# First and last routed expert stage: the two-round loop over experts written out over all units, with waits on constants

## The chip, the cores and the metric

The kernel runs on one core of one Trainium2 chip. The metric is the device time of one execution in microseconds (us), the median of several. The engines are named as the profile names them: PE is TensorE (matmul), PEld its weight loads, ACT is ScalarE, DVE is VectorE, POOL is GpSimd, SP is SyncE, which here only issues DMAs.

## What is computed

Four layers, each a cross attention and a gated feed-forward part. The change touches the feed-forward parts of the first and the last layer (L0 and L3), both mixtures of experts with two experts for each of 2048 tokens of 128 numbers. Cut to what matters, of the first (slots per expert: 640, experts: 8, hidden size 512):

```python
xe = zeros((E, cap + 1, D)).at[experts, pos_safe].set(xf[tokens])[:, :cap]
h = silu(einsum('ecd,edf->ecf', xe, W1)) * einsum('ecd,edf->ecf', xe, W3)
ye = einsum('ecf,efd->ecd', h, W2)
out = zeros((T, D)).at[tokens].add(wk[:, None] * ye[experts, ...])
```

and of the last (256 slots, 16 experts, hidden size 512):

```python
xin = einsum("tec,td->ecd", dispatch, xt)
h = gelu(einsum("ecd,edf->ecf", xin, fc1_w) + fc1_b[:, None, :], approximate=False)
eout = einsum("ecf,efd->ecd", h, fc2_w) + fc2_b[:, None, :]
```

## The kernel before

The whole network is one program. Its stages run one behind the other; each is a block in which every engine has its own list of instructions, engines wait for each other by counting semaphores, and a block ends when all engines have come to its end. `routed_experts` is the first routed stage (names `L0f_...`) and the last (`L3f_...`). The second one (`L2f_...`, function `block_experts`) is written another way and is not touched: straight code over 39 units, waits on constants.

A routed stage begins with the head (`lead`): gating, choosing experts, and sending every token's row to its expert's slots in DRAM (`slots`) by indirect DMAs of POOL. Then come the experts. An expert's slots are T tiles of 128 rows: five in the first stage, cut into units of three and of two tiles (`chunks=[3, 2]`), and two in the last, one unit (`chunks=[2]`). Weights and rows of U experts lie in SBUF at a time: U is 4 of 8 experts in the first stage, 8 of 16 in the last. The loop (`Fori`) over experts therefore makes two rounds, with U experts, and `UC` = 8 units, in its body. In both stages that is 16 units in all.

For a unit PE does three things, in functions of their names:

- `turn` (L2557): transposes the unit's rows into `psT`; ACT copies them into `xsT` (`turned`, L2513; in the last stage with scale and bias);
- `hidden` (L2566): for each of J = 4 column blocks one matmul into `psA`, in the first stage a second one into `psB` for the gate; ACT applies SiLU or GELU from `psA` into `h` (L2533), and in the first stage DVE multiplies `h` by `psB` (`gate`, L2617). `psA` and `psB` have two banks each, so the third column block waits until ACT has read the first (`a_free`);
- `outputs` (L2581): J matmuls for each tile into `psY`; DVE copies the result into `ys` (L2634, or with the bias L2632) and the rows' home addresses into `home` (L2630); POOL sends each tile of `ys` to its place in `results` by an indirect DMA (L2664).

Within a round these are pipelined by hand: PE issues unit k+2's `turn` and unit k+1's `hidden` ahead of unit k's `outputs`. The round starts with `turn(0)`, `turn(1)`, `hidden(0)` and ends with the `outputs` of its last two units, since `k + 2 < UC` and `k + 1 < UC` bound the pipeline to the body:

```python
for k in range(UC):
    if k + 2 < UC:
        turn(k + 2)
    if k + 1 < UC:
        hidden(k + 1)
    outputs(k)
```

Every wait in the body counts to a number that depends on the round (`i * UC + (k + 1)`), which each engine works out in a register. POOL's indirect DMAs follow a dummy multiply into `waited` (L2674), which waits for `y_free` (the copy) and for POOL's own counter `turn`. DVE's copy of a unit waits until the rows of the unit two before it have returned (`returned`), since `ys` has two buffers. SP loads the next round's rows and weights into an expert's place when its last unit has been copied (`y_free`, L2496 to L2498). ACT's function tables are loaded by instructions that the compiler puts in (`ACT_TABLE_LOAD`).

When all rows are back, the first stage fetches them for the next stage while PE computes the next attention's values (`Values1`); the last stage collects them and writes the output (`Collect`).

Of the kernel before, what the change touches and what calls it, by code (L numbers as in the profile page):

```python
# [18 lines left out]
P = 128  # L19
# [2396 lines left out]
def routed_experts(nc, m, name, c):  # L2416
# [6 lines left out]
    UC = U * CH  # L2423
    assert UC % 2 == 0 and UC >= 4 and EB % U == 0
    TOT = EB * CH
    NS = EB * T * P
# [9 lines left out]
    with ExitStack() as ctx:  # L2436
# [9 lines left out]
        pay, waited = c["last"] if ends else sb("pay", [P, 2, NT, PAY]), sb("waited", [P, 1])  # L2446
# [12 lines left out]
        turn = sem("turn")  # L2459
# [7 lines left out]
        N = UC * J  # L2467
# [3 lines left out]
        def _(sp):  # L2471
# [19 lines left out]
            with sp.Fori(0, EB // U - 1) as i:  # L2491
                for u in range(U):
                    at = lambda a: a[bass.ds(i * U + (U + u), 1)].rearrange(
                        "o p f -> p (o f)" if len(a.shape) == 3 else "o p j f -> p (o j) f")
# [12 lines left out]
        @block.scalar  # L2507
        def _(act):
            lead.scalar(act)
            with act.Fori(0, EB // U) as i:  # L2510
                a = Tally(N, i)

                def turned(k):  # L2513

                    tiles = units[k][2]
                    act.wait_ge(t_full, i * UC + (k + 1))

                    act.wait_ge(b_full, i * N + (k + 1) * J)
                    src, dst = psT[:, k % 2, 0:tiles * P], xsT[:, k % 2, 0:tiles * P]
                    if c.get("scale") is None:  # L2520
                        nc.scalar.copy(dst, src).then_inc(t_free, 1)  # L2521
                    else:
                        nc.scalar.activation(dst, src, ACT.Identity, bias=c["bias"], scale=c["scale"]).then_inc(t_free, 1)

                turned(0)
                turned(1)
                for k, (u, _, tiles) in enumerate(units):
                    for j in range(J):
                        if j == 0:

                            act.wait_ge(y_full, i * UC + (k + 1))
                        act.wait_ge(a_full, a.take() + (2 * J + 1))
                        nc.scalar.activation(h[:, k % 2, j, 0:tiles * P], psA[:, j % 2, 0:tiles * P], c["act"],  # L2533
                                             bias=b1s[:, u, j:j + 1] if b1 else 0.0).then_inc(a_free, 1)
                    if k + 2 < UC:
                        turned(k + 2)
                a.end()
            if values is not None:
                values.scalar(act)
            if ends:  # L2540
                collect.second(act)

        @block.tensor
        def _(pe):
# [9 lines left out]
            with pe.Fori(0, EB // U) as i:  # L2554
                a = Tally(N, i)

                def turn(k):  # L2557
                    u, first, tiles = units[k]
                    if first == 0:
                        pe.wait_ge(x_in[u], i * 16 + 16)  # L2560
                    pe.wait_ge(t_free, i * UC + (k + 1))
                    for t in range(tiles):
                        last = pe.transpose(psT[:, k % 2, t * P:(t + 1) * P], xs[:, u, first + t, 0:D], m.ident)
                    last.then_inc(t_full, 1)
# [30 lines left out]
                for k in range(UC):  # L2595
                    if k + 2 < UC:
                        turn(k + 2)
# [1293 lines left out]
```

## Time and profile before

| | us |
|---|---|
| median of 3 runs | 1281.98 |
| lowest and highest of them | 1275.63, 1286.26 |
| span of the profiled execution (no time of its own beside it) | 1279.7 |
| units of the first stage, from first transposes to last copy | 229.38 to 346.70 |
| units of the last stage, from first transposes to last copy | 1183.60 to 1260.72 |
| PE busy over the span | 1073.0 (84%) |
| DVE, ACT, POOL busy | 699.7, 600.8, 498.8 |
| mean granted clock of PE | 0.896 of full speed |

Times in the trace are counted from the span's start. Busy times are sums of an engine's instructions; PE's are modelled at their ends, since matmuls overlap. An entry in brackets behind a row is the engine's idle time before it and what ended it. In the table of stretches, each engine has its busy us and the number of its instructions.

### The profile page before, as it was taken

What the parts mean: (1) busy time and instruction counts of PE and PEld (TensorE: products, weight loads), DVE (VectorE), ACT (ScalarE), POOL (GpSimd) and SP (SyncE); (2) the same over time, 40 slices, a digit from 0 to 9 for tenths busy, and PEclk for the clock granted to TensorE, in tenths of its full rate; (3) what the DMA queues carried; (4) which work ended last, traced back from release to release, by engine and by line L of the source; (5) the groups of instructions that cost most, each with busy time, mean ns of one, the idle gap of its engine ahead of it and who ended that gap; (6) DMA issues with size and microseconds to landing.
All of it is one profiled execution on the core that took longest, in us unless ns stands there. A gap on an engine that the chain in (4) does not pass through costs nothing. (4 is left out here: it accounts for less than half of the span.)

```text
span 1279.7 us, 26365 instructions
## 1 busy us (share of the span) xinstructions
PE 1073.0 (84%) x8602; PEld 744.3 (58%) x8602; DVE 699.7 (55%) x3354; ACT 600.8 (47%) x1506; POOL 498.8 (39%) x783
## 2 busy tenths in 40 slices
PE   5999788799969999989996868994779999961983
PEld 4778565587725666664443655993644444541773
DVE  7667375233368776645465642115658888754012
ACT  3555466323257766624321432442644666631553
POOL 4767427133447565423003555551020000067343
PEclk9999799799979999998997975997876999975887
DMA  9789811131099950001660024662040222015533
GB/s 246 231 227 177 185 37 51 51 125 52 23 155 121 164 96 1 2 21 36 141 126 1 2 78 140 195 187 72 31 143 24 67 68 60 22 29 169 141 93 104
DMA packets 138791, 124.60 MB, mean 97 GB/s; under 512 B 14015, under 2 KB 112737, under 8 KB 138665
## 3 DMA queue, kind: packets, MB, share of 16 engines
q1 hardware_dynamic: 129624, 107.82, 36.7%
q0 software_dynamic: 7168, 12.83, 3.0%
q10 hardware_dynamic: 1872, 2.37, 0.5%
q8 instruction: 67, 1.10, 0.4%
q14 instruction: 60, 0.48, 0.1%
HBM read 88.12 MB, written 37.70 MB: 98 GB/s over the span
## 5 line engine op out<-in xcount | busy, mean ns | idle before, releaser
L998 ACT ACTIVATE L_Z<-L_Z,L_nmx 128x154 f32<-128x154 f32 x256 | 105.2, 412 | 47.9 <-DVE L_nmx L1071 47.7
L3592 DVE CUSTOM_DVE_ANT_0 L3s_masked<-L3s_psS,L3s_trilw 128x512 f32<-128x512 f32 (+3 forms) x256 | 109.8, 486 | 24.0 <-PE L3s_psS L3419 23.5
L347 POOL TENSOR_TENSOR L_Z<-L_Z,L_mx 128x512 f32<-128x512 f32 x84 | 87.6, 1043 | 63.9 <-DVE L_mx L722 62.0
L3547 ACT ACTIVATE L3s_E<-L3s_psT 128x512 f32<-128x512 f32 (+1 forms) x192 | 87.6, 529 | 49.2 <-PE L3s_psT L3432 49.0
L887 POOL TENSOR_TENSOR L_Z<-L_Z,L_rin 128x488 f32<-128x488 f32 x64 | 64.1, 1001 | 67.2 <-DVE L_rin L1079 67.2
L912 PE MATMUL L_psS<-L1k_G,L_xnT 128*128 128x462 f32 x192 | 84.7, 539 | 4.8 <-DVE L_nmx L1071 3.5
L722 DVE CUSTOM_DVE_ANT_0 L_Z<-L_psS,L_Z 128x154 f32<-128x154 f32 x256 | 63.4, 313 | 31.1 <-PE L_psS L403 28.6
L1071 DVE CUSTOM_DVE_ANT_0 L_Z<-L_psS,L_mask 128x154 f32<-128x154 f32 x256 | 67.7, 311 | 11.9 <-PE L_psS L912 9.4
L578 ACT ACTIVATE L_E<-L_psT 128x512 f32<-128x512 f32 x84 | 46.2, 596 | 53.7 <-PE L_psT L416 53.6
L1089 DVE COPY L_PT<-L_psT 122x512 f32<-122x512 f32 x64 | 43.7, 683 | 38.5 <-PE L_psT L922 38.2
L3389 POOL COPY L3s_VG<-L3s_V 128x236 f32<-128x236 f32 x16 | 6.1, 386 | 149.5 <-PE L3s_psO L3443 148.2
L3419 PE MATMUL L3s_psS<-L3s_KS,L3s_QS 72*128 72x512 bf16 (+3 forms) x256 | 55.6, 333 | 7.7 <-PEq L3405 4.6
L2617 DVE TENSOR_TENSOR L0f_h<-L0f_h,L0f_psB 128x384 f32<-128x384 f32 (+1 forms) x64 | 31.2, 488 | 54.2 <-PE L0f_psB L2579 50.4
L3430 PE MATMUL L3s_psT<-L3s_QS,L3s_KS 75*128 75x512 bf16 (+3 forms) x256 | 60.3, 313 | 0.0
L3443 PE MATMUL L3s_psO<-L3s_E,L3s_VG 128*32 128x128 f32 (+3 forms) x512 | 49.6, 452 | 8.3 <-ACT L3s_E L3547 8.1
L2841 POOL DMA_INDIRECT resultsL<-L2f_ys,L2f_home x39 | 38.1, 977 | 44.9 <-DVE L2f_ys L2828 44.6
L3430 PEld LDWEIGHTS L3s_psT<-L3s_QS,L3s_KS 75*128 75x128 bf16 x256 | 25.8, 101 | 44.9 <-issue 23.1
L2576 PE MATMUL L0f_psA<-L0f_xsT,L0f_w 128*128 128x256 f32 (+1 forms) x128 | 47.0, 450 | 3.4 <-ACT L0f_xsT L2521 3.4
L3432 PE MATMUL L3s_psT<-L3s_triub,L3s_identb 128*128 128x128 bf16 x256 | 48.2, 225 | 0.0
L1403 ACT ACTIVATE L1m_h<-L1m_psA 128x512 f32<-128x512 f32 x36 | 21.4, 598 | 56.6 <-PE L1m_psA L1317 56.5
L416 PE MATMUL L_psT<-const,L_Z 128*128 128x128 f32 x336 | 47.4, 287 | 0.5 <-ACT L_Er L578 0.5
L998 ACT ACTIVATION_READ_ACCUMULATOR L_Z<-L_Z,L_nmx 128x1 f32 x256 | 47.8, 187 | 0.0
(638 smaller groups left out, 2812.1 us busy)
## 6 DMA issues: line engine op xcount, KB each, us to landing
L_Z<-in_fside_Bx16xSxS SPq DMA_DIRECT2D x16, 1232.0 KB, 7.1
L2f_w<-in_L_ffn_W SPq DMA_DIRECT2D x39, 256.0 KB, 3.4
slotsL<-empty SPq DMA_DIRECT2D x1, 8320.5 KB, 75.1
L3f_w<-in_L_ffn_fc_w SPq DMA_DIRECT2D x32, 256.0 KB, 4.1
L0f_w<-in_L_ffn_W SPq DMA_DIRECT2D x24, 256.0 KB, 3.9
L1m_cb<-comb_rows SPq DMA_DIRECT2D x6, 1024.0 KB, 10.1
L3s_QS<-q_parts SPq DMA_DIRECT2D x144, 32.0 KB
L3s_KS<-k_parts SPq DMA_DIRECT2D x48, 96.0 KB
```

Of the source, the lines that this page charges most:

```text
L347: nc.gpsimd.tensor_tensor(Z[:, t % NZ, h, 0:KM_], Z[:, t % NZ, h, 0:KM_], top.broadcast_to([P, HG, KM_]), ALU.subtract).then_inc(z_ready, 1)
L722: last = nc.vector.tensor_tensor_reduce(Z[:, t % NZ, h], psS[:, j, (g % 3) * S2:(g % 3) * S2 + S2], add, 1.0, LOW, ALU.add, ALU.max, mx[:, ...
L887: nc.gpsimd.tensor_tensor(zz, zz, r.unsqueeze(2).broadcast_to([P, 4, KM]), ALU.mult).then_inc(norm_done, 1)
L912: pe.matmul(psS[:, n % 2, 0:w * S2], xnT[:, (t // 2) % 2, (t % 2) * P:(t % 2 + 1) * P], G[:, t // TB, hs].rearrange("p h k -> p (h k)"), s ...
L998: last = nc.scalar.activation(Z[:, t % 2, h], Z[:, t % 2, h], ACT.Exp, scale=-1.0, bias=nmx[:, t % 2, h:h + 1], accum_out=sums[:, t % 2, h ...
L1071: last = nc.vector.tensor_tensor_reduce(Z[:, t % 2, h], psS[:, n % 2, at:at + S2], mask[:, t % TB], 1.0, -LOW, ALU.add, ALU.min, nmx[:, t ...
L3419: last = pe.matmul(psS[:, k, at:at + wd], QS[0:TR, g.slot, h, t * P:(t + 1) * P], KS[0:TR, g.slot, h, 0:wd], start=(n == 0), stop=(n == le ...
L3430: pe.matmul(psT[:, k, at:at + wd], KS[0:TR + 3, g.slot, h, t * P:(t + 1) * P], QS[0:TR + 3, g.slot, h, t * P:S], start=(n == 0), stop=Fals ...
L3432: last = pe.matmul(psT[:, k, at:at + P], identb[:], triub[:], start=False, stop=(n == len(tiles) - 1), skip_group_check=True)
L3443: last = pe.matmul(psO[32 * h:32 * h + 32, j * P:S], VG[:, g.par, j, h * (DH + 1):h * (DH + 1) + 32], E[:, g.par, h, EO[j]:EO[j] + S - j * ...
L3547: nc.scalar.activation(E[:, g.par, h, EO[group[0]]:EO[group[0]] + wd], psT[:, k, 0:wd], ACT.Exp).then_inc(t_free, 1)
L3592: last = nc.vector.tensor_tensor_reduce(masked[:, k, at:at + wd], psS[:, k, at:at + wd], trilw[:, S - wd:S], 1.0, LOW, ALU.add, ALU.max, m ...
```

## The change

The body of the loop becomes plain code over all 16 units n of a stage: `units` runs over all experts, `e % U` names an expert's place in SBUF, the pipeline runs through (`n + 2 < TOT`), and every wait is for a constant. The dummy multiply, its tile and the counter `turn` go. SP's loads, of the same sizes under the same counts, are written out as well. The core of the diff (DVE's part changes in the same way as PE's):

```diff
-    units = [(u, sum(chunks[:q]), chunks[q]) for u in range(U) for q in range(CH)]
+    units = [(e, sum(chunks[:q]), chunks[q]) for e in range(EB) for q in range(CH)]
...
-            with sp.Fori(0, EB // U - 1) as i:
-                for u in range(U):
...
-                    sp.wait_ge(y_free, i * UC + ((u + 1) * CH + 2))
-                    sp.dma_start(xs[:, u], at(slots_in)).then_inc(x_in[u], 16)
-                    load_w(at, u)
+            for e in range(U, EB):
+                sp.wait_ge(y_free, (e - U + 1) * CH + 2)
+                sp.dma_start(xs[:, e % U], slots_in[e]).then_inc(x_in[e % U], 16)
+                load_w(lambda a: a[e], e % U)
...
-            with act.Fori(0, EB // U) as i:
-                a = Tally(N, i)
...
+            def turned(n):
+                e, _, tiles = units[n]
+                act.wait_ge(t_full, n + 1)
+                act.wait_ge(b_full, (n + 1) * J)
...
+            turned(0)
+            turned(1)
+            for n, (e, _, tiles) in enumerate(units):
+                act.wait_ge(y_full, n + 1)
+                for j in range(J):
+                    act.wait_ge(a_full, n * J + j + 2 * J + 1)
+                    nc.scalar.activation(h[:, n % 2, j, 0:tiles * P], psA[:, j % 2, 0:tiles * P], c["act"],
+                                         bias=b1s[:, e % U, j:j + 1] if b1 else 0.0).then_inc(a_free, 1)
+                if n + 2 < TOT:
+                    turned(n + 2)
...
-            with pe.Fori(0, EB // U) as i:
...
-                for k in range(UC):
-                    if k + 2 < UC:
-                        turn(k + 2)
-                    if k + 1 < UC:
-                        hidden(k + 1)
-                    outputs(k)
-                a.end()
+            turn(0)
+            turn(1)
+            hidden(0)
+            for n in range(TOT):
+                if n + 2 < TOT:
+                    turn(n + 2)
+                if n + 1 < TOT:
+                    hidden(n + 1)
+                outputs(n)
...
-            pool.sem_inc(turn, 1)
-            with pool.Fori(0, EB // U) as i:
-                for k in range(UC):
-                    pool.wait_ge(turn, i * UC + (k + 1))
-                    pool.wait_ge(y_free, i * UC + (k + 3))
-
-                    nc.gpsimd.tensor_tensor(waited[:], m.ones[:, 0:1], m.ones[:, 0:1], ALU.mult).then_inc(turn, 1)
-                    give_back(k)
+            for n, (e, first, tiles) in enumerate(units):
+                pool.wait_ge(y_free, n + 3)
...
```

Two places of the order of instructions follow. The first is ACT at the start of the first stage's units, the list of before: behind the routing's exponential come the loop's branch and the body, in which a table load stands in front of the first copy (behind the wait for the transposes, `t_full`) and one in front of the first SiLU (behind a wait for `y_full` alone).

```order
L1663 ACTIVATE L0f_e<-L0f_e 128x16 [waits L0f_diff_ready]
L2510 UNCONDITIONAL_BRANCH
L2510 ISA
L2518 ISA [waits L0f_t_full]
L2521 ACT_TABLE_LOAD
L2521 COPY L0f_xsT<-L0f_psT 128x384 [waits L0f_b_full]
L2516 REGISTER_ALU
L2518 REGISTER_ALU [waits L0f_t_full]
L2521 COPY L0f_xsT<-L0f_psT 128x256 [waits L0f_b_full]
L2532 REGISTER_ALU [waits L0f_y_full]
L2533 ACT_TABLE_LOAD
L2533 ACTIVATE L0f_h<-L0f_psA 128x384 [waits L0f_a_full]
```

The same place in the list of the change.

```order
L1663 ACTIVATE L0f_e<-L0f_e 128x16 [waits L0f_diff_ready]
L2510 COPY L0f_xsT<-L0f_psT 128x384 [waits L0f_b_full,L0f_t_full]
L2510 COPY L0f_xsT<-L0f_psT 128x256 [waits L0f_b_full,L0f_t_full]
L2520 ACT_TABLE_LOAD [waits L0f_a_full]
L2520 ACTIVATE L0f_h<-L0f_psA 128x384 [waits L0f_y_full]
L2520 ACTIVATE L0f_h<-L0f_psA 128x384 [waits L0f_a_full] x3
```

The load in front of the copies is gone; the one in front of the SiLU now waits for the first hidden result (`a_full`). The part between the branch and the loop's end was run twice, and with it its two loads. In the last stage the order is the same, with GELU.

The second place is PE at the end of the last stage's units, the list of before: the end of the loop's body, the outputs of its last two units back to back, then the branch back.

```order
L2576 MATMUL L3f_psA<-L3f_xsT,L3f_w 128x256
L2587 MATMUL L3f_psY<-L3f_w,L3f_h 128x128 x8
L2583 REGISTER_ALU
L2587 MATMUL L3f_psY<-L3f_w,L3f_h 128x128 x8
L2554 REGISTER_ALU
L2554 COMPARE_AND_BRANCH
L2436 UNCONDITIONAL_BRANCH
```

The same place in the list of the change, from the transposes of unit 15 on.

```order
L2547 MATMUL L3f_psT<-const,L3f_xs 128x128 x2
L2559 MATMUL L3f_psA<-L3f_xsT,L3f_w 128x256 x4
L2570 MATMUL L3f_psY<-L3f_w,L3f_h 128x128 x8
L2559 MATMUL L3f_psA<-L3f_xsT,L3f_w 128x256 x4
L2570 MATMUL L3f_psY<-L3f_w,L3f_h 128x128 x16
L2435 UNCONDITIONAL_BRANCH
```

Before, the sixteen output matmuls back to back stood behind units 6 and 7 and again behind units 14 and 15; now only behind units 14 and 15, and between units 7 and 8 stands what stands between any two units: transposes, a hidden layer, outputs.

## Rows read from the trace of the kernel before

**Rows 1.** Table of stretches: busy us of PE, PEld, DVE, ACT, POOL; clock, DMA share, GB/s

```profile
289.40:291.90 2.50, 0.71 (x8) 0.48 (x5) 0.49 (x2) 1.93 (x3) 1.89 (x3) 1.00 0.35 63
...
291.90:352.00 60.10, 60.10 (x330) 46.02 (x331) 20.95 (x50) 20.23 (x45) 24.25 (x32) 1.00 0.11 37
...
1192.00:1221.80 29.80, 28.89 (x194) 24.77 (x194) 3.46 (x14) 14.43 (x33) 13.91 (x20) 1.00 0.61 169
...
1221.80:1225.90 4.10, 1.19 (x6) 0.70 (x5) 0.49 (x2) 4.06 (x6) 3.14 (x5) 0.87 0.82 196
...
1225.90:1231.70 5.80, 5.80 (x15) 4.20 (x16) 0.00 (x0) 3.18 (x7) 0.22 (x1) 0.50 0.43 150
...
800.00:868.00 68.00, 68.00 (x612) 68.00 (x611) 12.52 (x72) 31.06 (x72) 34.85 (x36) 1.00 0.63 180
```

**Rows 2.** Timeline of VectorE, first stage: start, us, copies of finished units 0, 4, 8

```profile
247.40 0.55 DVE L2634 COPY L0f_ys<-L0f_psY 128x384 f32<-128x384 f32 x1
...
274.64 0.55 DVE L2634 COPY L0f_ys<-L0f_psY 128x384 f32<-128x384 f32 x1
...
303.96 0.55 DVE L2634 COPY L0f_ys<-L0f_psY 128x384 f32<-128x384 f32 x1
```

**Rows 3.** The same of the last stage: copies of units 0, 5, 8

```profile
1195.14 0.42 DVE L2632 TENSOR_TENSOR L3f_ys<-L3f_psY,L3f_b 128x256 f32<-128x256 f32 x1
...
1215.90 0.42 DVE L2632 TENSOR_TENSOR L3f_ys<-L3f_psY,L3f_b 128x256 f32<-128x256 f32 x1
...
1233.84 0.42 DVE L2632 TENSOR_TENSOR L3f_ys<-L3f_psY,L3f_b 128x256 f32<-128x256 f32 x1
```

**Rows 4.** Timeline of ACT and PE at the first stage's back edge

```profile
289.96 1.28 ACT L2521 ACT_TABLE_LOAD   x1 [4.91 <-PE L0f_psT L2563]
...
291.86 0.91 PE L2576 MATMUL L0f_psA<-L0f_xsT,L0f_w 128*128 128x384 f32 x2 [1.79 <-ACT L0f_xsT L2521]
```

**Rows 5.** Timeline of PE and ACT at the last stage's back edge

```profile
1223.71 1.13 PE L2576 MATMUL L3f_psA<-L3f_xsT,L3f_w 128*128 128x256 f32 x4 [1.87 <-ACT L3f_xsT L2523]
...
1224.05 1.28 ACT L2533 ACT_TABLE_LOAD   x1
...
1225.88 0.80 PE L2576 MATMUL L3f_psA<-L3f_xsT,L3f_w 128*128 128x256 f32 x1 [1.04 <-ACT L3f_h L2533]
```

**Rows 6.** Timeline at the first stage's start: table load, first and third hidden column block

```profile
230.38 1.28 ACT L2521 ACT_TABLE_LOAD   x1 [7.44 <-PE L0f_psT L2563]
...
232.29 1.64 PE L2576 MATMUL L0f_psA<-L0f_xsT,L0f_w 128*128 128x384 f32 x2 [1.58 <-ACT L0f_xsT L2521]
...
237.56 1.23 PE L2576 MATMUL L0f_psA<-L0f_xsT,L0f_w 128*128 128x384 f32 x2
```

**Rows 7.** Timeline at the last stage's start: first hidden matmuls, GELU, third matmul

```profile
1186.38 1.22 PE L2576 MATMUL L3f_psA<-L3f_xsT,L3f_w 128*128 128x256 f32 x2 [1.56 <-ACT L3f_xsT L2523]
...
1188.02 0.94 ACT L2533 ACTIVATE L3f_h<-L3f_psA,L3f_b 128x256 f32<-128x256 f32 x2
...
1188.55 1.22 PE L2576 MATMUL L3f_psA<-L3f_xsT,L3f_w 128*128 128x256 f32 x2
```

**Rows 8.** Timeline of copies and return issues: last stage, then second routed stage

```profile
1199.29 0.42 DVE L2632 TENSOR_TENSOR L3f_ys<-L3f_psY,L3f_b 128x256 f32<-128x256 f32 x1
...
1200.49 0.99 POOL L2664 DMA_INDIRECT resultsL<-L3f_ys,L3f_home  x1 [0.51 <-issue]
...
1262.00 0.22 POOL L2674 TENSOR_TENSOR L3f_waited<-const 128x1 f32<-128x1 f32 x1
...
811.32 0.28 DVE L2828 COPY L2f_ys<-L2f_psY 128x128 f32<-128x128 f32 x1
...
812.37 0.98 POOL L2841 DMA_INDIRECT resultsL<-L2f_ys,L2f_home  x1 [0.92 <-DVE L2f_ys L2828]
```

**Rows 9.** Last stage: landing of returns (view by tile); its weight loads (DMA view)

```profile
DMA to landing us min/median/max: 2.1/2.9/4.6
...
L3f_w<-in_L_ffn_fc_w SPq DMA_DIRECT2D x16, 256.0 KB, 3.2
```

More of the change, by code:

```diff
@@ L2445, in routed_experts @@
         ends = c["key"] == "L3"
-        pay, waited = c["last"] if ends else sb("pay", [P, 2, NT, PAY]), sb("waited", [P, 1])
+        pay = c["last"] if ends else sb("pay", [P, 2, NT, PAY])
         xs, xsT = sb("xs", [P, U, T, PAY]), sb("xsT", [P, 2, NMAX])
@@ L2509, in _ @@
             lead.scalar(act)
-            with act.Fori(0, EB // U) as i:
-                a = Tally(N, i)
[L2513 to L2534, printed above, removed]
-                    if k + 2 < UC:
-                        turned(k + 2)
-                a.end()
+            def turned(n):
+                e, _, tiles = units[n]
+                act.wait_ge(t_full, n + 1)
+                act.wait_ge(b_full, (n + 1) * J)
+                src, dst = psT[:, n % 2, 0:tiles * P], xsT[:, n % 2, 0:tiles * P]
+                if c.get("scale") is None:
+                    nc.scalar.copy(dst, src).then_inc(t_free, 1)
+                else:
+                    nc.scalar.activation(dst, src, ACT.Identity, bias=c["bias"], scale=c["scale"]).then_inc(t_free, 1)
+            turned(0)
[8 more added lines that the diff above has]
+                    turned(n + 2)
             if values is not None:
@@ new lines, in turn, with hidden @@
+            def turn(n):
+                e, first, tiles = units[n]
+                if first == 0:
+                    pe.wait_ge(x_in[e % U], 16 * (e // U + 1))
+                pe.wait_ge(t_free, n + 1)
+                for t in range(tiles):
+                    last = pe.transpose(psT[:, n % 2, t * P:(t + 1) * P], xs[:, e % U, first + t, 0:D], m.ident)
+                last.then_inc(t_full, 1)
+            def hidden(n):
+                e, first, tiles = units[n]
+                u, w = e % U, tiles * P
+                if first == 0:
+                    pe.wait_ge(w_in[u], 16 * nw * (e // U + 1))
+                pe.wait_ge(t_free, n + 3)
+                x = xsT[:, n % 2, 0:w]
+                for j in range(J):
+                    pe.wait_ge(a_free, n * J + j + 1)
+                    pe.matmul(psA[:, j % 2, 0:w], w1[:, u, j * P:(j + 1) * P], x, start=True, stop=True).then_inc(a_full, 1)
+                    if glu:
+                        pe.wait_ge(b_free, n * J + j + 1)
+                        pe.matmul(psB[:, j % 2, 0:w], w3[:, u, j * P:(j + 1) * P], x, start=True, stop=True).then_inc(b_full, 1)
@@ new lines, in outputs @@
+            def outputs(n):
+                e, first, tiles = units[n]
+                pe.wait_ge(b_free, (n + 1) * J + 2)
+                pe.wait_ge(y_free, n + 1)
+                for t in range(tiles):
+                    for j in range(J):
+                        last = pe.matmul(psY[:, n % 2, t * P:(t + 1) * P], h[:, n % 2, j, t * P:(t + 1) * P], w2[:, e % U, j],
+                                         start=(t == 0 and j == 0), stop=(t == tiles - 1 and j == J - 1),
+                                         skip_group_check=True)
+                last.then_inc(y_full, 1)
```

99 lines of the change are left out of this document (25 added, 74 removed).

## The prediction

> **What bounds the kernel now.** I read the table of stretches first, for which engine fills the two routed stages and at what clock; then the vector engine's copies of finished units in order of time, which are the pulse of each stage; then the scalar and tensor engines' timeline at the three places where a stage's loop begins or begins again.
>
> In the table of stretches the reader is to see that TensorE (PE) is the bound of both stages, except in a hole in the middle. In the last stage PE is busy 28.89 of 29.80 us at a granted clock of 1.00 before the hole, 1.19 of 4.10 us in it, and then 5.80 of 5.80 us at 0.50, the lower of its two levels (1.2 GHz against 2.4) [rows 1]. So what a change gains outside the hole is at most the 0.91 us of PE's idle time per round.
>
> The pulse says what the hole costs. In the first stage units alternate between three and two tiles; unit 0 is copied at 247.40 and unit 4 at 274.64, so a pair takes 13.62 us. Unit 8, the first of round two, would be due two pairs after unit 4, at 301.88, and comes at 303.96: 2.08 us late [rows 2]. In the last stage units 0 and 5 are copied at 1195.14 and 1215.90, so a unit takes 4.152 us. Unit 8 would be due at 1195.14 + 8 x 4.152 = 1228.36 and comes at 1233.84: 5.48 us late [rows 3].
>
> The timeline names the cause. At the back edge PE has run the last two units' outputs and can only transpose; ScalarE (ACT) first loads an activation table, then copies, and only then PE's next hidden layer starts. In the first stage that is one idle stretch of 1.79 us [rows 4]. In the last stage there are two, 1.87 and 1.04 us, the second behind a second table load of 1.28 us that the GELU waits for; and after them comes the stretch at half clock [rows 1, 5].
>
> **The change part by part.**
>
> *The round boundary.* Written out, PE issues unit 8's transposes and hidden layer ahead of unit 6's and 7's outputs, as between any two units. The lateness of unit 8 is what goes: 2.08 us in the first stage, 5.48 us in the last. I take both whole, since the pulse holds every cost of the boundary (idle, table loads, branch, clock) whatever its share. For the last stage the lower bound is the case in which the clock would not have fallen in a typical execution: 5.80 us of work at half clock would then have taken 2.90, and the boundary would be worth 5.48 - 2.90 = 2.58 us. I stay with 5.48, the measured one.
>
> *The stage's start.* Before, the loop body begins with its own table load, which waits for the first transposes and holds up the first copy. In the change ACT copies with the table that the routing left, and that load is gone. In the first stage PE's first hidden layer starts 0.63 us after the end of the load (230.38 + 1.28 = 231.66) [rows 6]; without it everything there moves forward by 1.28 us. But the second load, for SiLU or GELU, moves: before, it ran as soon as the copies were done; now it also waits for the first hidden result. In the first stage that is covered: the result comes 1.64 us after the start of the hidden layer, so at 231.01 + 1.64 = 232.65, the load ends at 233.93, and the matmul that needs the SiLU behind it would start at 237.56 - 1.28 = 236.28, 2.3 us later [rows 6]. Gain 1.28 us. In the last stage tiles are smaller and it is not covered: the hidden layer starts at 1186.38 - 1.28 = 1185.10, its first result is there 1.22 us later, at 1186.32; load and GELU take 1.28 + 0.47 and end at 1188.07; the third matmul, 0.06 us behind, starts at 1188.13 to 1188.15, against 1188.55 now [rows 7]. Gain 0.4 us. I count 1.68 for the two; if the moved load were covered in both it would be 2.56, and if in neither, 0.8.
>
> By the Trainium skill ("ScalarE: Activation LUTs", What ACT_TABLE_LOAD costs) a switch of tables costs about 1.28 us plus a drain of about 1.38, or 2.66. By that the first stage's start would be worth 2.66 and the sum 1.4 us more. The trace shows no drain around the load: it ends at 231.66 and PE, which waits for the copy behind it, runs at 232.29; so the sum goes by 1.28.
>
> *GpSimd's dummy multiply* (`waited`) and its `turn` counter. It lasts 0.22 us in the row shown, yet from the end of the vector copy (1199.29 + 0.42) to the DMA issue behind it take 0.78 us; in the second routed stage, where GpSimd waits for the copy directly, the same way takes 811.32 + 0.28 to 812.37, or 0.77 us [rows 8]. So nothing comes of it while the queue is idle. In each stage's tail the queue is busy and one multiply stands in it; I count 0.1 us for each stage, between 0 and 0.2.
>
> *Constants for register sums.* PE's idle 0.91 us per round of the last stage is the most that this could give there, 1.8 us; in the first stage PE is busy 60.10 of 60.10 us and has none to give [rows 1]. The second routed stage already waits on constants in straight code and PE is busy 68.00 of 68.00 us [rows 1], so straight code as such costs PE nothing visible. I take 0.
>
> *SyncE's loads* keep their conditions (the same counts of finished units), so they come as early relative to the units as before. Expert 8's weights are asked for when unit 0 is copied and land about 3.2 us later [rows 9]; its unit is transposed some 24 us later than that. What is next late is PE's own work.
>
> **The sum.** 1.28 + 2.08 + 0.1 in the first stage, 0.4 + 5.48 + 0.1 in the last: 9.4 us. Everything behind the first stage waits for its last returns, so it shifts as a whole; the last stage's tail does too. The profiled execution has a span of 1279.7 us, with no separate time of its own; it lies 2.3 us below the median of the three runs (1281.98; 1275.63 to 1286.26), inside them. Taken off the median: 1272.6 us.
>
> **The rivals.**
>
> *Half clock is not part of it* (the gain is smaller). For it: in the first stage a hole of 1.79 us left the clock at 1.00 [rows 1, 4], so holes near that size are on the edge, and other executions may never have lost the clock in the last stage. Against: here there are two holes close together. Gain 9.4 - 2.9 = 6.5, time 1275.5.
>
> *More than the sum* (the gain passes 1%). PE starts sooner after its transposes in both stages, so the clock may rise sooner. It rose between 4.3 us (last stage) and 6.1 us (first) after the first hidden matmul in this execution; as early as 4.3 in the first stage would save half of 1.8, 0.9 us. With the 1.8 us of constants, and 0.9 if the last stage's moved load is covered after all: 9.4 + 3.6 = 13.0, time 1269.0. Each piece has a row against it or is a coin toss.
>
> *Slower: the returns become the bound of the last stage.* A unit's copy waits for the return of the unit two before it. One cycle is copy 0.42 + 0.78 to the first issue + 0.99 for that issue + landing of 2.9 us in the median, 4.6 at most [rows 8, 9]: 5.1, at worst 6.8, against two units or 8.3 us. It decides once landings pass 6.1 us. If they doubled from their worst to 9.2, a unit would take 11.4 / 2 = 5.7 instead of 4.15 us, 25 us over 16 units; less 9.4 that is 15 slower, 1297. Against it: these landings were measured while weights for the next round were flowing, as they will be.
>
> *The change does not do what it says*: unit 8's rows or weights are not there and the hole stays, leaving the starts and tails, 1.9 us, 1280. The landing times above speak against it.
>
> **How the numbers follow.** Forecast, 8 to 11 us: 0.56. Half clock not part: 0.20. More than the sum: 0.15, of which some ends short of 1%. Slower: 0.04. Not done: 0.05. One per cent is 12.8 us, about what a measurement of this kernel can tell from no change. Faster by over 1%: 0.17 (the third case and the forecast's edge); slower by over 1%: 0.04; within: 0.79. The range runs from 1265 (the larger case with a run's scatter of some 4 us, from the spread of the three runs) to 1279 (the smaller case with the same scatter).
>
> **What would show it.** Right: in the pulse, unit 8 one unit's time behind unit 7 (4.15 us; a pair of 13.6) in both stages; two table loads fewer at each boundary and one at each start; no stretch at 0.50 in the middle of the last stage; the last stage's third hidden matmul held by a table load that starts after PE's first result. The starts are wrong if PE's first hidden layer stays more than 2 us behind the transposes. The whole is wrong if the pulse itself changes from 13.62 and 4.15, or if the tails grow.

## The result and the profile after

| | before | after |
|---|---|---|
| median of 8 runs, us | 1282.05 | 1272.54 |
| lowest and highest, us | 1275.63, 1286.26 | 1268.41, 1276.10 |
| ratio of the two, 95% interval | | 0.9941, 0.9918 to 0.9965 |

By the medians the change takes 9.5 us off, by the ratio 7.6 (4.5 to 10.5): less than the one per cent that counts as faster, and distinctly more than nothing. Predicted were 1272.6 us and, as the likeliest case (0.79), a change within 1%. That the sum is so close does not show that its terms are, so they are taken one by one below.

The page after: the span, PE's row, then the two other engines that the change touches.

```profile
span 1272.7 us, 25924 instructions
...
PE 1075.3 (84%) x8602; PEld 747.2 (59%) x8602; DVE 697.3 (55%) x3354; ACT 592.4 (47%) x1500; POOL 490.8 (39%) x751
```

PE's 8602 instructions are the same in number; ACT has six fewer than the 1506 of before (all table loads: 6 x 1.28 = 7.7 of the 600.8 - 592.4 = 8.4 us of busy time that it lost), POOL 32 fewer than 783 (the dummy multiplies). So the change did what it says. In PE's rows each matmul of a hidden layer or of the outputs counts as two instructions (a transpose as one): the four matmuls of a hidden layer of the last stage are x8, and "the third matmul" is the third column block.

The pulse of both stages, as in [rows 2, 3]: VectorE's timeline, copies of units 0, 4 and 8 of the first stage and 0, 5 and 8 of the last.

```profile
247.96 0.55 DVE L2612 COPY L0f_ys<-L0f_psY 128x384 f32<-128x384 f32 x1
...
275.22 0.55 DVE L2612 COPY L0f_ys<-L0f_psY 128x384 f32<-128x384 f32 x1
...
302.47 0.55 DVE L2612 COPY L0f_ys<-L0f_psY 128x384 f32<-128x384 f32 x1
...
1193.27 0.42 DVE L2610 TENSOR_TENSOR L3f_ys<-L3f_psY,L3f_b 128x256 f32<-128x256 f32 x1
...
1214.23 0.42 DVE L2610 TENSOR_TENSOR L3f_ys<-L3f_psY,L3f_b 128x256 f32<-128x256 f32 x1
...
1226.81 0.42 DVE L2610 TENSOR_TENSOR L3f_ys<-L3f_psY,L3f_b 128x256 f32<-128x256 f32 x1
```

In the first stage a pair takes (275.22 - 247.96) / 2 = 13.63 us, and unit 8 would be due at 275.22 + 27.26 = 302.48: it comes at 302.47. In the last stage a unit takes (1214.23 - 1193.27) / 5 = 4.192 us, unit 8 is due at 1193.27 + 33.54 = 1226.81 and comes then. The lateness of unit 8, 2.08 and 5.48 us before, is gone to the hundredth. What is new is the pulse of the last stage itself: 4.192 instead of 4.152 us.

The table of stretches shows the same for PE: busy us of PE, PEld, DVE, ACT and POOL with their instructions, then clock, DMA share and GB/s; the old boundary of the first stage, then all units of the last, then its old boundary.

```profile
290.00:352.00 62.00, 62.00 (x353) 47.38 (x352) 21.44 (x53) 19.72 (x44) 24.27 (x25) 1.00 0.13 41
1191.00:1250.00 59.00, 56.31 (x367) 48.19 (x366) 6.92 (x28) 31.45 (x71) 26.22 (x27) 1.00 0.43 115
1213.00:1223.00 10.00, 9.62 (x67) 8.41 (x67) 1.45 (x6) 4.73 (x11) 4.36 (x5) 1.00 0.78 200
1223.00:1231.00 8.00, 7.62 (x52) 6.51 (x51) 0.60 (x5) 4.24 (x10) 3.88 (x4) 1.00 0.56 152
```

Where before stood 1.19 of 4.10 us and then 5.80 us at a clock of 0.50 [rows 1], PE is now busy 7.62 of 8.00 at 1.00, no less than its neighbours. The 2.69 us that it idles between 1191 and 1250 lie in every unit, a little under 0.2 us each.

**Stage by stage.** The spans of two executions differ by more than this change. Each is therefore cut at three rows: the first transposes of a stage, its copy of unit 0 and its copy of unit 15, all as in [rows 2, 3]. The parts that the change touches add up as follows (us):

| | first: transposes to copy 0 | copy 0 to copy 15 | last: transposes to copy 0 | copy 0 to copy 15 | sum | all else in the span |
|---|---|---|---|---|---|---|
| before | 18.02 | 98.88 | 11.54 | 65.16 | 193.60 | 1086.1 |
| after | 14.71 | 96.84 | 11.49 | 60.26 | 183.30 | 1089.4 |
| gain | 3.31 | 2.04 | 0.05 | 4.90 | 10.30 | -3.3 |

All else is code that the change leaves as it was, apart from the two tails. In the ten executions of this study it ran from 1078.0 to 1096.2 us, 18 us, without order between kernels: it is the scatter of a run. For instance the code ahead of the first stage ended at 233.25 us after and 229.38 before. So terms are read from the columns of the two stages, and whole times from medians and ratios only.

### The profile page after: what moved, and what is told of

Same layout as the page of the kernel before. It is cut to its first block and busy times, and to the rows that moved or that the text cites. A ratio compares the mean times of both kernels' runs of the same rounds, so it can differ in the third digit from the quotient of the medians.

```text
span 1272.7 us, 25924 instructions
## 1 busy us (share of the span) xinstructions
PE 1075.3 (84%) x8602; PEld 747.2 (59%) x8602; DVE 697.3 (55%) x3354; ACT 592.4 (47%) x1500; POOL 490.8 (39%) x751
## 5 line engine op out<-in xcount | busy, mean ns | idle before, releaser
L2640 POOL DMA_INDIRECT resultsL<-L0f_ys,L0f_home x40 | 38.8, 971 | 82.4 <-DVE L0f_ys L2612 74.8
L2808 POOL DMA_INDIRECT resultsL<-L2f_ys,L2f_home x39 | 38.0, 974 | 46.1 <-DVE L2f_ys L2795 45.8
L2640 POOL DMA_INDIRECT resultsL<-L3f_ys,L3f_home x32 | 31.1, 971 | 48.3 <-DVE L3f_ys L2610 43.4
```

The source lines that it names most:

```text
L2640: pool.indirect_dma_start(results, bass.IndirectOffsetOnAxis(ap=home[:, e % U, first + t:first + t + 1], axis=0), ys[:, n % 2, t], None, b ...
```

## The experiments

The theory was the prediction's sum: at the boundaries the drained pipeline, the table loads and the half clock; at the starts the table load. The first rival was that the straight code as such, constants instead of register sums, carries the gain; the second that the two stages do not add. Of the kernels below the first three were timed against 22 runs of before (median 1279.63) and the last against 11 (1278.74); four had one execution each, for their traces. The median of before was 1282.05, 1279.63 and 1278.74 us in its three sets of runs, so each time is compared with its own set alone. The four columns of the table above for all of them, and how late unit 8 comes after what the pulse before it makes due:

| | first: to copy 0 | 0 to 15 | unit 8 late | last: to copy 0 | 0 to 15 | unit's time | unit 8 late | sum | median or single time |
|---|---|---|---|---|---|---|---|---|---|
| before | 18.02 | 98.88 | 2.08 | 11.54 | 65.16 | 4.152 | 5.48 | 193.60 | 1282.05 |
| after | 14.71 | 96.84 | -0.01 | 11.49 | 60.26 | 4.192 | 0.00 | 183.30 | 1272.54 |
| e1 first stage only | 15.25 | 96.84 | -0.01 | 11.71 | 65.30 | 4.150 | 5.64 | 189.10 | 1278.62 |
| e2 last stage only | 17.75 | 98.88 | 2.06 | 11.37 | 60.26 | 4.192 | 0.00 | 188.26 | 1275.70 |
| e3 loop, table ahead | 14.85 | 97.60 | 0.79 | 9.53 | 60.66 | 4.152 | 0.98 | 182.64 | 1268.29 |
| e4 straight, drained | 15.21 | 97.47 | 0.64 | 11.74 | 61.22 | 4.192 | 0.96 | 185.64 | 1265.49 (one) |
| e5 table ahead | 15.39 | 96.84 | 0.00 | 9.70 | 60.26 | 4.192 | 0.00 | 182.19 | 1270.66 (one) |
| e6 one wait less | 14.67 | 96.84 | 0.02 | 11.07 | 59.75 | 4.154 | 0.00 | 182.33 | 1279.29 (one) |
| e7 four banks | 14.72 | 96.84 | 0.00 | 9.06 | 53.81 | 3.730 | 0.01 | 174.43 | 1262.23 (one) |
| e8 e5 to e7 together | 14.66 | 96.84 | 0.01 | 8.78 | 53.81 | 3.732 | 0.00 | 174.09 | 1264.12 |

**e1 and e2: one stage at a time.** The function of before is kept beside the new one under another name, and one of the two stages calls it (here e1; e2 is the mirror of it).

```diff
-        routed_experts(nc, m, "L3f"
+        routed_experts_loop(nc, m, "L3f"
```

> The first routed stage as in the change, the last as before. Theory (the terms are separate and add): first stage from first to last copied unit 96.8 us (98.9 before), last stage 65.2 us if PE's clock falls at its back edge again, about 62.3 if it does not; the time lies 3 to 5 us below before, at 1277 to 1279. Rival (the gain is one whole, most of it not from the stages' own holes): less than 2 or more than 7 us.

> The last routed stage as in the change, the first as before. Theory (separate terms): first stage 98.9 us from first to last copied unit, last stage 60.3; the time lies 5 to 6.5 us below before, at about 1276. Rival: less than 3 us, the rest needing the first stage's change as well.

Measured: e1 1278.62 us, ratio 0.9985 (0.9956 to 1.0014); e2 1275.70, ratio 0.9959 (0.9924 to 0.9995). In the traces each stage is as in the kernel that it comes from, and the gains, 4.50 (193.60 - 189.10) and 5.34, add up to 9.84 of the 10.30. By its ratio e2 gains 5.2 us, as its trace says; e1 gains 1.9, less than the 3 to 5 expected, with an interval from 5.6 gained to 1.8 lost, which holds the 4.5 of the trace without showing it. In the traces the stages add, and neither helps or hinders the other; the whole times (1.9 and 5.2 us, 7.6 for both) agree with this, though their middles lie below the gains of the traces.

e1 also answers whether the half clock was a chance of the one execution seen before. The old boundary of its last stage, in the timeline of ACT and PE, and a stretch behind it (columns as in the table of stretches above):

```profile
1222.34 1.28 ACT L2751 ACT_TABLE_LOAD   x1 [3.38 <-PE L3f_psT L2791]
...
1224.33 1.12 PE L2804 MATMUL L3f_psA<-L3f_xsT,L3f_w 128*128 128x256 f32 x4 [1.88 <-ACT L3f_xsT L2751]
...
1226.50 2.07 PE L2804 MATMUL L3f_psA<-L3f_xsT,L3f_w 128*128 128x256 f32 x4 [1.04 <-ACT L3f_h L2761]
```

```profile
1226.00:1232.00 6.00, 5.50 (x14) 3.98 (x15) 0.00 (x0) 3.55 (x8) 0.55 (x1) 0.50 0.51 179
```

The two holes of [rows 5] are there again (1.88 and 1.04 us, before 1.87 and 1.04), and the clock falls to 0.50 again. So it fell in both traces of the old boundary; the executions without a trace cannot say.

**e3: the loop of before, its table loaded early.** One small activation at the head of the loop's body makes the compiler load the SiLU or GELU table there; the copies behind it need no load of their own.

```diff
                 a = Tally(N, i)
+                nc.scalar.activation(warm[:], m.ones[:, 0:1], c["act"])
```

> The kernel before with its loops and register waits, and one added 128x1 SiLU or GELU at the head of ACT's loop body that waits for nothing, so that the one table load of the body runs while PE still computes the last outputs. Theory (the hole at the back edge is the table loads, and in the last stage the half clock behind them): the hole shrinks to about 0.8 us in the first stage (unit 8 about 302.7 against a due time of 301.9, counted as in the kernel before) and to under 1 us in the last, where the clock stays at 1.00; first to last copied unit 97.6 and 60.7 us; the kernel gains most of what the change gains, 7 us or more. Rival (the hole is the drained pipeline, or the branch and the register sums): the holes stay at 1.5 us or more and 3 us or more, the gain under 3 us.

Measured: 1268.29 us, ratio 0.9909 (0.9879 to 0.9939): 11.6 us, as much as the change or more, with the loop, the register waits, the dummy multiply and the drained pipeline all kept. The boundaries in the timeline, first stage (PE's hidden layer of unit 8), then last (outputs of units 6 and 7, load, hidden layer, copy of unit 8):

```profile
291.56 0.91 PE L2578 MATMUL L0f_psA<-L0f_xsT,L0f_w 128*128 128x384 f32 x2 [0.50 <-ACT L0f_xsT L2523]
...
1210.49 3.73 PE L2589 MATMUL L3f_psY<-L3f_w,L3f_h 128*128 128x128 f32 x32
...
1211.18 1.28 ACT L2513 ACT_TABLE_LOAD   x1
...
1215.26 2.39 PE L2578 MATMUL L3f_psA<-L3f_xsT,L3f_w 128*128 128x256 f32 x8 [0.59 <-ACT L3f_xsT L2525]
...
1222.17 0.42 DVE L2634 TENSOR_TENSOR L3f_ys<-L3f_psY,L3f_b 128x256 f32<-128x256 f32 x1
```

The load now runs at 1211.18, beside the 3.73 us of the outputs of units 6 and 7. PE's hole is 0.50 us in the first stage instead of 1.79, and 0.59 in the last instead of 1.87 and 1.04; the second is gone, and the clock stays at its higher level:

```profile
1213.00:1223.00 10.00, 9.14 (x55) 6.93 (x54) 1.05 (x5) 5.78 (x13) 4.52 (x7) 1.00 0.71 204
```

So of the first boundary's 2.08 us the table load is 1.29 and the drained pipeline 0.79; of the last one's 5.48, the loads with the half clock that followed are 4.50 and the drained pipeline 0.98. How the 4.50 divide between the two is not shown. The rival, that constants carry the gain, falls: the loop without the loads is as fast as the straight code.

**e4: straight code, drained after unit 7.** The converse. Unit 8's and 9's transposes and unit 8's hidden layer are put behind unit 7's outputs; ACT's and DVE's steps follow suit.

```diff
-                if n + 2 < TOT:
+                if n + 2 < TOT and n not in (6, 7):
                     turn(n + 2)
-                if n + 1 < TOT:
+                if n + 1 < TOT and n != 7:
                     hidden(n + 1)
                 outputs(n)
+                if n == 7:
+                    turn(8)
+                    turn(9)
+                    hidden(8)
```

> The change, but with the pipeline drained after unit 7 as the loop did: units 8 and 9 are transposed and unit 8's hidden layer issued only behind unit 7's outputs; straight code, constants, no table load there. Theory (table loads): unit 8 comes 0.5 to 0.9 us late in the first stage and 0.3 to 1 us late in the last, and the clock stays at 1.00. Rival (the drained pipeline itself costs the hole): 1.5 us or more late in the first stage, 2.5 us or more in the last.

Measured: unit 8 is 0.64 us late in the first stage and 0.96 in the last (copies at 1183.17, 1204.13 and 1217.67: due at 1183.17 + 8 x 4.192 = 1216.71).

```profile
1183.17 0.42 DVE L2617 TENSOR_TENSOR L3f_ys<-L3f_psY,L3f_b 128x256 f32<-128x256 f32 x1
...
1204.13 0.42 DVE L2617 TENSOR_TENSOR L3f_ys<-L3f_psY,L3f_b 128x256 f32<-128x256 f32 x1
...
1210.69 1.10 PE L2562 MATMUL L3f_psA<-L3f_xsT,L3f_w 128*128 128x256 f32 x4 [0.48 <-issue]
...
1217.67 0.42 DVE L2617 TENSOR_TENSOR L3f_ys<-L3f_psY,L3f_b 128x256 f32<-128x256 f32 x1
```

The two ways of draining, with a loop and without one, cost 0.79 and 0.64 in the first stage and 0.98 and 0.96 in the last: by this comparison the branch back and the register sums add at most 0.15 us. Its single time of 1265.49 says nothing on this: all else took 1078.0 us in that execution, the least of the ten.

**e5: the change, with the table loaded ahead of the first copy.** The start of the last stage is where the prediction left a load on the path.

```diff
+            nc.scalar.activation(warm[:], m.ones[:, 0:1], c["act"])
             turned(0)
             turned(1)
```

> The change, and ACT runs one 128x1 SiLU or GELU behind the routing's exponential, before it waits for the first transposes, so that the table load that the change moved behind PE's first hidden result runs in ACT's idle time. Theory (the moved load is covered in the first stage and uncovered in the last): the first stage's start, from first transposes to first copied unit, stays at 14.7 to 15.3 us, the last stage's falls from 11.5 to about 9.5 to 10.5, and PE's idle time of 1.05 us ahead of its third hidden matmul falls to 0.3 or less. Rival (the load costs nothing in the last stage either, since the clock sets the start): the last stage's start stays above 11.

Measured: 9.70 us from the transposes to copy 0 in the last stage, against 11.49. PE runs its eight hidden matmuls without a hole, and ACT's first GELU follows its result:

```profile
1180.91 3.89 PE L2561 MATMUL L3f_psA<-L3f_xsT,L3f_w 128*128 128x256 f32 x8
...
1182.19 0.47 ACT L2522 ACTIVATE L3f_h<-L3f_psA,L3f_b 128x256 f32<-128x256 f32 x1 [0.64 <-PE L3f_psA L2561]
```

The hole was 1.05 us and the gain is 1.79. The rest goes with the clock, which rose 5.2 us after the first transposes instead of 7.8: less the hole, that is 7.8 - 1.05 - 5.2 = 1.6 us less of work at half clock, by estimate worth half, 0.8 us. In the first stage it gave nothing (15.39 against 14.71; e1 and e4, without it, have 15.25 and 15.21), as the load there was covered.

**e6: the change without ACT's wait for the outputs.** This is about the unexpected 0.04 us in each unit of the last stage. In the loop ACT waited for `y_full` by an instruction of its own, the register sum; in the straight code the activation has to wait for two things, `y_full` and the hidden result. ACT's order, with what each waits for (first stage, unit 2; the last has the same); the experiment leaves the first of the two lines with `a_full` alone:

```
L2520 ACTIVATE L0f_h<-L0f_psA 128x384 [waits L0f_a_full,L0f_y_full]
L2520 ACTIVATE L0f_h<-L0f_psA 128x384 [waits L0f_a_full] x3
```

```diff
-                act.wait_ge(y_full, n + 1)
+                if n == TOT - 1:
+                    act.wait_ge(y_full, n + 1)
                 for j in range(J):
```

> The change without ACT's wait for y_full ahead of a unit's first SiLU or GELU (implied by the transposes that ACT has waited for already, except for the last unit, where it stays). Theory (a unit of the last stage became 0.04 us longer, 4.19 against 4.15, since that wait now stands with a second one on the activation itself, where the loop had it on a register instruction run ahead): 4.15 us per unit, PE's idle time ahead of the third hidden matmul 0.15 instead of 0.19. Rival (the straight code or constants on other instructions): 4.19 as in the change.

Measured: the unit is back at 4.154 us, 59.75 instead of 60.26 from copy 0 to copy 15. Behind unit 0, ACT's copy of the next transposes and the hidden layer after the change, first and third matmul with ACT's rows between them:

```profile
1193.21 1.03 PE L2559 MATMUL L3f_psA<-L3f_xsT,L3f_w 128*128 128x256 f32 x4
...
1193.41 0.56 ACT L2512 ACTIVATE L3f_xsT<-L3f_psT,cols 128x256 f32<-128x256 f32 x1 [1.53 <-PE L3f_psT L2547]
...
1193.91 0.84 ACT L2520 ACTIVATE L3f_h<-L3f_psA,L3f_b 128x256 f32<-128x256 f32 x2
...
1194.43 1.13 PE L2559 MATMUL L3f_psA<-L3f_xsT,L3f_w 128*128 128x256 f32 x4 [0.19 <-ACT L3f_h L2520]
```

The same in e6, with its start of the stage (copies, load, third matmul) ahead of it:

```profile
1187.75 1.12 ACT L2512 ACTIVATE L3f_xsT<-L3f_psT,cols 128x256 f32<-128x256 f32 x2 [13.05 <-PE L3f_psT L2548]
...
1188.89 1.28 ACT L2521 ACT_TABLE_LOAD   x1
...
1190.71 2.08 PE L2560 MATMUL L3f_psA<-L3f_xsT,L3f_w 128*128 128x256 f32 x4 [0.26 <-ACT L3f_h L2521]
...
1198.23 0.56 ACT L2512 ACTIVATE L3f_xsT<-L3f_psT,cols 128x256 f32<-128x256 f32 x1 [1.53 <-PE L3f_psT L2548]
...
1198.69 0.88 ACT L2521 ACTIVATE L3f_h<-L3f_psA,L3f_b 128x256 f32<-128x256 f32 x2
...
1199.21 1.13 PE L2560 MATMUL L3f_psA<-L3f_xsT,L3f_w 128*128 128x256 f32 x4 [0.15 <-ACT L3f_h L2521]
```

The GELU starts 0.50 us after ACT's copy before it with two waits (1193.41 to 1193.91) and 0.46 after it with one (1198.23 to 1198.69); the trace of the change has a wait instruction of ACT (L2519) between the two, that of e6 has none. PE idles 0.15 instead of 0.19 us. With e3, whose register waits also give 4.152, this says that constants were neither dearer nor cheaper than registers: the second wait on the activation was dearer. The first three rows of e6 show a second effect: with one wait on the first GELU the table load in front of it runs directly behind the copies (1188.87 to 1188.89), so PE's hole at the start is 0.26 us instead of 1.05. That is worth less than in e5: the clock still rose only 8.0 us after the first transposes, and copy 0 comes after 11.07 us, where e5 has 9.70.

**e7: four banks for `psA` in the last stage.** PE's 0.19 us in each unit stand in front of the third matmul, which waits until ACT has read one of the two banks (`a_free`). The last stage has no `psB`, so two more banks are there. ACT's reads follow (`psA[:, j % NA]`).

```diff
-        psT, psA, psY = ps("psT", [P, 2, 512]), ps("psA", [P, 2, 512]), ps("psY", [P, 2, 512])
+        NA = 2 if glu else 4
+        psT, psA, psY = ps("psT", [P, 2, 512]), ps("psA", [P, NA, 512]), ps("psY", [P, 2, 512])
...
-                pe.sem_inc(a_free, 2)
+                pe.sem_inc(a_free, NA)
...
-                    pe.matmul(psA[:, j % 2, 0:w], w1[:, u, j * P:(j + 1) * P], x, start=True, stop=True).then_inc(a_full, 1)
+                    pe.matmul(psA[:, j % NA, 0:w], w1[:, u, j * P:(j + 1) * P], x, start=True, stop=True).then_inc(a_full, 1)
...
-                pe.wait_ge(b_free, (n + 1) * J + 2)
+                pe.wait_ge(b_free, (n + 1) * J + NA)
```

> The change with four psA banks in the last stage instead of two (PSUM has two free there), so that PE's third and fourth hidden matmul of a unit wait for no GELU. Theory (behind the hole, the last stage's pulse is PE's stream of 3.8 us plus that wait): 3.8 to 3.9 us per unit instead of 4.19, first to last copied unit 55 to 57 us instead of 60.3. Rival (ACT or the returns are next): 4.05 or more.

Measured: a unit takes 3.73 us, less than expected; copy 0 to copy 15 is 53.81 us, and the start 9.06. The table of stretches, eight units of e7:

```profile
1187.25:1217.10 29.85, 29.85 (x210) 28.20 (x209) 3.95 (x17) 17.62 (x40) 15.54 (x16) 1.00 0.73 206
```

and six units after the change:

```profile
1193.21:1218.36 25.15, 24.00 (x158) 20.53 (x157) 2.97 (x13) 13.46 (x30) 11.65 (x12) 1.00 0.68 183
```

PE is now busy 29.85 of 29.85 us. Of the 0.46 us that a unit gained (4.192 - 3.730) only 0.19 had been idle time (25.15 - 24.00, over six units). The other 0.27 stood in PE's rows as busy: a unit's eight hidden matmuls, as two rows of four with the wait between them, lasted 1.03 + 1.13 = 2.16 us (the rows shown with e6), and as one row of eight they last 1.89:

```profile
1187.25 1.89 PE L2560 MATMUL L3f_psA<-L3f_xsT,L3f_w 128*128 128x256 f32 x8
```

The ends of PE's rows are modelled, and here a row that ends at a wait shows more busy time than the same matmuls in an unbroken row. The bound of the prediction on what a change could gain outside the hole, "the 0.91 us of PE's idle time per round" or 1.8 in all, was for this reason too low: e7's pulse is 0.42 us under the loop's 4.152, 6.3 us over the 15 units behind unit 0.

**e8: e5, e6 and e7 together.**

> The three together: table loaded ahead, no y_full wait, four banks in the last stage. Theory: they add; last stage from first transposes to last copied unit 63 to 66 us (76.7 before, 71.8 in the change), first stage 111 to 113; 14 to 17 us below before, ratio 0.987 to 0.989. Rival (the gain is lost in the tail, where POOL issues two returns of 1.3 us per unit): the last stage's tail grows by 2 us or more, ratio above 0.991.

Measured: 1264.12 us in the median of 6 runs (1255.75 to 1272.12), ratio to before 0.9886 (0.9840 to 0.9933). The last stage takes 62.59 us, a little less than expected, but only 0.28 less than e7 alone, in whose trace PE already runs the stage's first eight hidden matmuls and the units behind them without a hole: with four banks the load and the second wait are covered by PE's own matmuls. So the three do not add. The rival falls: from copy 15 to the end of the span take 19.50 us, before 19.39. The stages of the trace gain 19.5 us (193.60 - 174.09), more than the 14.6 of the whole times, whose interval (8.6 to 20.5) holds both. This is the fastest version that was timed with an interval. It beats both kernels: before by 14.6 us, and the change by 9.2 us of stage time (183.30 - 174.09); against the change itself the interval is not direct, since both were measured against before.

## Why the prediction was right, point by point

**First stage's start: 1.28 predicted, 3.31 measured.** The mechanism is the one named: the first load is gone, the second moved behind the hidden result, and is covered: the third matmul follows without idle time. The margin is smaller than the 2.3 us of the prediction, since PE was sooner at full clock: the first of the two SiLUs ends some 0.4 us ahead of the matmul. Timeline after the change, transposes, hidden layer, load, SiLU, third matmul into `psA`:

```profile
233.25 1.33 PE L2547 MATMUL L0f_psT<-const,L0f_xs 128*128 128x128 f32 x5 [8.08 <-DMA L0f_xs<-slotsL]
...
234.77 1.62 PE L2559 MATMUL L0f_psA<-L0f_xsT,L0f_w 128*128 128x384 f32 x2 [0.19 <-issue]
...
236.47 1.28 ACT L2520 ACT_TABLE_LOAD   x1 [1.48 <-PE L0f_psA L2559]
...
237.76 0.93 ACT L2520 ACTIVATE L0f_h<-L0f_psA 128x384 f32<-128x384 f32 x2
...
238.64 0.81 PE L2559 MATMUL L0f_psA<-L0f_xsT,L0f_w 128*128 128x384 f32 x2
```

The hidden layer starts 1.52 us behind the first transposes, where it was 2.91 (232.29 [rows 6] less 229.38): 1.39 for the load, the predicted 1.28 and 0.11 more. The other 1.92 us lie between the start of the hidden layer and copy 0, where PE is never idle in either trace, and go with the clock. Stretches after the change,

```profile
234.00:237.00 3.00, 2.81 (x7) 1.53 (x6) 0.00 (x0) 1.33 (x3) 0.00 (x0) 0.50 0.53 191
237.00:238.00 1.00, 1.00 (x4) 0.54 (x3) 0.00 (x0) 0.99 (x2) 0.00 (x0) 0.88 0.00 0
```

and before:

```profile
237.00:238.00 1.00, 1.00 (x3) 0.60 (x2) 0.19 (x1) 0.02 (x1) 0.00 (x0) 0.50 0.00 0
238.00:239.00 1.00, 1.00 (x4) 0.53 (x3) 0.36 (x1) 0.17 (x1) 0.00 (x0) 0.79 0.00 0
```

A mean of 0.88 between 0.50 and 1.00 means that the clock rose 0.24 us into that microsecond, at 237.24, or 4.0 us after the first transposes; before, at 238.42 by the same reckoning, or 9.0 us after them, with a hole of 1.58 us [rows 6] behind the transposes. So of its hidden layer PE had 2.5 us at half clock (234.77 to 237.24) instead of 6.1 (232.29 to 238.42), and half of the difference is 1.8 of the 1.92 us. This term was mis-sized: the prediction had it only as a part of "more than the sum", priced at 0.9 and judged a coin toss. It is there in every trace in which the load is out of the way, but not at one size: to copy 0 take 14.66 to 15.39 us, against 17.75 and 18.02 with the load. So the gain is 2.4 to 3.4 us, and this pair of traces is near the upper end.

**The boundaries: 2.08 and 5.48 predicted.** Unit 8 is on time in both. From copy 0 to copy 15 the gains are 2.04 and 4.90, the second less by the slower pulse below. That the measured lateness was taken whole, half clock included, was right for the traces: against the case "half clock is not part of it" stands that e1 lost the clock again, the second time of two. The prediction named the idle, the loads, the branch and the clock together and did not divide them; e3 and e4 did, and the loads are most of it.

**Last stage's start: 0.4 predicted, 0.05 measured.** The path to the third matmul is as worked out:

```profile
1181.78 1.11 PE L2547 MATMUL L3f_psT<-const,L3f_xs 128*128 128x128 f32 x4 [18.66 <-DMA L3f_xs<-slotsL]
...
1183.17 2.04 PE L2559 MATMUL L3f_psA<-L3f_xsT,L3f_w 128*128 128x256 f32 x4 [0.28 <-issue]
...
1184.44 1.28 ACT L2520 ACT_TABLE_LOAD   x1 [0.91 <-PE L3f_psA L2559]
...
1185.73 0.84 ACT L2520 ACTIVATE L3f_h<-L3f_psA,L3f_b 128x256 f32<-128x256 f32 x2
...
1186.26 2.08 PE L2559 MATMUL L3f_psA<-L3f_xsT,L3f_w 128*128 128x256 f32 x4 [1.05 <-ACT L3f_h L2520]
```

The load waits for PE's first result, and the third matmul starts 4.48 us behind the transposes instead of 4.95 (1188.55 [rows 7] less 1183.60): 0.47 gained. But a hole of 1.05 us now lies between hidden matmuls, and the clock rises later:

```profile
1182.00:1189.00 7.00, 5.67 (x16) 3.73 (x16) 0.00 (x0) 4.24 (x8) 0.00 (x0) 0.50 0.37 103
1189.00:1190.00 1.00, 1.00 (x4) 0.59 (x2) 0.00 (x0) 0.65 (x2) 0.00 (x0) 0.72 0.00 0
```

By the mean of 0.72 that is at 1189.56, 7.8 us after the transposes, where before it was 7.1. Behind the third matmul PE then has 3.3 us at half clock instead of 2.2, which by estimate takes 0.56 us back. That the later clock comes of the hole's place is not shown. The step that failed is "Gain 0.4 us", which took a gain at the third matmul for one at the copy. No gain at the copy is clear of the scatter: it comes after 11.54 and 11.71 us with the old start (before, e1) and after 11.37, 11.49 and 11.74 with the new one (e2, after, e4). e5, which has no hole there, shows what the load still cost: 1.79 us.

The rows of the load also bear on what the prediction weighed from the Trainium skill ("ScalarE: Activation LUTs", What ACT_TABLE_LOAD costs), a load of about 1.28 us and a drain of about 1.38. The load starts at 1184.44 and the GELU at 1185.73, 1.29 us later: 1.28 of load and 0.01 of anything else; in e6 the copies ahead of the load end 0.02 us before it. No run here shows the drain; with it the first stage's hidden layer would have gained 2.66, and it gained 1.39.

**Constants: 0 predicted, -0.5 measured.** The pulse of the first stage stayed (13.62 and 13.63). In the last stage 4.192 against 4.152 cost about 0.5 us in all (60.26 - 59.75, e6). The prediction looked at registers against constants and had not seen that the wait for `y_full` moves onto the activation, though the order of instructions shows it. By its own words a changed pulse would make "the whole" wrong; at 1% of one stage's pulse it made one term wrong.

**GpSimd's multiply: 0 when idle, 0.1 for each tail.** In the timeline after the change, from the copy to the DMA issue behind it:

```profile
1197.46 0.42 DVE L2610 TENSOR_TENSOR L3f_ys<-L3f_psY,L3f_b 128x256 f32<-128x256 f32 x1
...
1198.65 0.97 POOL L2640 DMA_INDIRECT resultsL<-L3f_ys,L3f_home  x1 [1.94 <-DVE L3f_ys L2610]
```

1198.65 - 1197.88 = 0.77 us, where it was 0.78 with the multiply [rows 8]: nothing. The tail of the last stage, from copy 15 to the end of the span, went from 19.39 to 19.15 us, which agrees with 0.1 and cannot show it.

**The returns as a bound** fell: they land in 2.1 to 4.8 us after the change, median 3.3 (before 2.9 and at most 4.6, [rows 9]), by the view of that tile, against the 6.1 from which the rival decides. With four banks they come to 5.6 at most.

**The sum.** Terms of 9.24 without the tails became 10.30: 2.03 more at the first start, 0.35 less at the last, 0.04 and 0.58 less in the two bodies. Errors of both signs partly cancelled, and that the median came within 0.1 us of the forecast is luck: the first start alone differs by 0.7 us between traces of the new code. The median moved by 9.5 us and the ratio by 7.6; the ratio's interval (4.5 to 10.5 us) holds 9.24 and 10.30. So the mechanism is shown by the traces, and of the whole time only the range.

## What to carry to other kernels

Where a loop's boundary costs more than its drained pipeline should, look first for what the compiler put into the body: here a function-table load at the head of every round was 1.29 of 2.08 us in one stage, and in the other the loads and the half clock behind them were 4.5 of 5.48. One activation placed ahead of the copies gave as much as writing out the whole loop (0.9909 against 0.9941, intervals overlapping). When straight code is made from a loop, look in the order at which instruction each wait now stands on, and judge a short wait of PE by a trial with more banks rather than by its idle time, which showed less than half of it.

## What the runs showed that was not expected

- A second wait on an activation delayed PE by 0.04 us per unit (idle 0.19 against 0.15 us; 4.192 against 4.154 us for a unit). All four traces of the straight last stage with both waits and two banks have 4.192 (after, e2, e4, e5); the loops and e6 have 4.150 to 4.154.
- A table load in front of an activation with two waits took over one of them and ran only when that was met (1184.44, behind PE's result); in front of one with a single wait it ran directly behind the copies (1188.89 in e6).
- PE's clock rose later behind a long hole in the first microseconds of a stage, but the length of the hole is not all. In e5 it rose, by the stretch below and the same reckoning, at 1184.70, 5.2 us after its first transposes (1179.52). In the last stage it took 4.5 to 5.2 us in e3, e5, e7 and e8, with no hole over 0.32 us, and 7.1 to 8.3 in the five traces with a hole of 1.05 to 1.67; but e6, whose longest hole is 0.26, took 8.0. In the first stage it took 3.9 to 5.4 us with a hole of at most 0.30 and 8.5 and 9.0 with one of 1.58. What decides is not shown.

```profile
1180.00:1185.00 5.00, 4.94 (x14) 3.17 (x14) 0.00 (x0) 2.71 (x6) 0.00 (x0) 0.53 0.47 133
```

- Holes of 0.59 us (e3) and 0.48 us (e4) at the last stage's boundary left the clock at 1.00, and so did one of 1.79 us in the first stage [rows 1, 4]; two close together, of 1.87 or 1.88 and 1.04 us, were followed by 0.50 both times. What of them decides was not tried.
- Code that no kernel here changes took between 1078.0 and 1096.2 us from one execution to the next. Where that comes from stays open; it is why a single time says nothing on terms of a few microseconds.
